# A hybrid block on one core: the table that orders the attention's steps on four engines is drawn anew

## What is computed

```python
x = x + attention(layernorm(x))   # gated delta rule, 16 heads of 128x128, short convolutions
x = x + ffn(layernorm(x))         # silu(x Wg) * (x Wu), 1024 hidden, then Wd
x = x + mamba(layernorm(x))       # 512 channels, 16 states, a scan over time
x = x + ffn(layernorm(x))
```

```python
q, k, v = (silu(short_conv(h @ W)) for W in (Wq, Wk, Wv))   # 4 taps; then q and k are normalised
g = exp(-softplus(h @ Wfa @ Wfb + dt_bias) * exp(A_log)); beta = sigmoid(h @ Wb)
# for every token t, with a 128x128 state S:
S = S * g[t]; delta = (v[t] - k[t] @ S) * beta[t]; S = S + outer(k[t], delta); o[t] = q[t] @ S
out = (rmsnorm(o) * norm_w * sigmoid(h @ Wga @ Wgb)) @ Wo
```

## Time and profile before

| | |
|---|---|
| median of three runs | 2769.22 us (2768.93 to 2771.27) |
| profiled execution | 2776.06 us |
| its span, first to last instruction | 2774.3 us |
| TensorE busy | 2495.6 us (90%), 46,512 matmul records |
| VectorE busy | 2124.1 us (77%) |
| ScalarE busy | 1393.4 us (50%) |
| GpSimd busy | 1260.3 us (45%) |
| mean granted TensorE clock | 0.966 |

### The profile page before, as it was taken

How to read it: one execution, slowest core, us unless ns; L and a number is a source line. 1 busy time by engine, 2 the same in 40 slices (tenths; PEclk the granted TensorE clock), 3 DMA queues, 4 the chain that set the end, 5 groups by cost and what they waited for, 6 DMA issues and landing times.

```text
span 2774.3 us, 102732 instructions
## 1 busy us (share of the span) xinstructions
PE 2495.6 (90%) x46512; PEld 1483.1 (53%) x46512; DVE 2124.1 (77%) x3249; ACT 1393.4 (50%) x2647; POOL 1260.3 (45%) x989
## 2 busy tenths in 40 slices
PE   6799999999999999999999999989878889888888
PEld 3466666666666566666666666664323333333333
DVE  3778888888888787888888877863229989999981
ACT  3445555455545455455555554533255645556342
POOL 0545545555555444555555454540014645546540
PEclk9899999999999999999999999999989999999999
DMA  1000000000000000000000000010012323323320
GB/s 52 22 12 14 13 20 13 15 13 20 13 16 13 13 20 13 16 13 20 13 15 15 18 13 15 7 52 1 25 38 92 126 92 112 112 90 127 121 95 15
DMA packets 52069, 105.61 MB, mean 38 GB/s; under 512 B 7084, under 2 KB 11948, under 8 KB 51376
## 3 DMA queue, kind: packets, MB, share of 16 engines
q1 hardware_dynamic: 51632, 99.04, 11.0%
HBM read 96.65 MB, written 2.37 MB: 36 GB/s over the span
## 4 chain that ended last, share of the span: by engine, by line
PE 60%; DVE 15%; issue 12%; ACT 11%; POOL 1%; DMA 1%; SPq 0%; DVEq 0%; ACTq 0%; POOLq 0%
PE bank L359 8%; PE bank L461 5%; DVE hs L1683 5%; PE bank L609 4%; PE bank L424 4%; PE pair L577 3%; PE bank L1500 3%; PE pair L567 3%; PE bank L393 2%; PE bank L583 2%; PE bank L549 2%; PE bank L531 2%; PE bank L1422 2%; PE bank L572 2%; DVE cv L651 2%
## 5 line engine op out<-in xcount | busy, mean ns | idle before, releaser
L1989 POOL TENSOR_TENSOR dBu<-dtu,Bn 128x1024 f32<-128x1024 f32 x128 | 306.2, 2394 | 232.1 <-DVE hc L1690 231.8
L651 DVE SCALAR_TENSOR_TENSOR cv<-raw,taps,cv 128x1024 f32<-128x1024 f32 x288 | 385.1, 1338 | 16.4 <-ACT cv L917 14.0
L359 PE MATMUL bank<-xn,W 128*128 128x512 f32 x768 | 381.9, 621 | 0.0
L1176 POOL TENSOR_TENSOR kL<-kL,tot 128x512 f32<-128x512 f32 x128 | 195.2, 1525 | 258.0 <-PE bank L424 258.0
L916 ACT ACTIVATE raw<-bank 128x512 f32<-128x512 f32 x192 | 114.9, 599 | 370.9 <-PE bank L359 370.1
L1500 PE MATMUL bank<-hc,eye 128*128 128x512 f32 x512 | 249.1, 615 | 56.2 <-DVE hc L1690 56.1
L1887 ACT ACTIVATE bank<-dtv,m_A 128x512 f32<-128x512 f32 x256 | 174.3, 687 | 209.6 <-DVE hs L1683 208.8
L1151 POOL TENSOR_TENSOR R<-qn,gate 128x1024 f32<-128x1024 f32 x32 | 108.6, 3393 | 269.5 <-ACT gate L977 269.5
L1500 PEld LDWEIGHTS bank<-hc,eye 128*128 128x128 f32 x512 | 93.7, 193 | 201.8 <-DVE hc L1690 110.6
L359 PEld LDWEIGHTS bank<-xn,W 128*128 128x128 f32 x768 | 132.3, 191 | 112.9 <-issue 103.0
L1690 DVE TENSOR_TENSOR hc<-hs,Cn 128x1024 f32<-128x1024 f32 x128 | 171.9, 1343 | 11.5 <-PE bank L1500 7.3
(11 more groups left out here) (267 smaller groups left out, 5657.4 us busy)
## 6 DMA issues: line engine op xcount, KB each, us to landing
Bn<-ssm_rows SPq DMA_DIRECT2D x128, 256.0 KB, 3.5
Cn<-ssm_rows SPq DMA_DIRECT2D x128, 256.0 KB, 3.2
W<-in_head_w SPq DMA_DIRECT2D x32, 448.0 KB, 3.3
WO<-in_out_w SPq DMA_DIRECT2D x32, 192.0 KB, 2.3
xT<-in_xT SPq DMA_DIRECT2D x1, 2048.0 KB, 8.1
out_xT<-xT SPq DMA_DIRECT2D x4, 512.0 KB, 3.8
xn<-in_w_gate SPq DMA_DIRECT2D x1, 1024.0 KB, 5.8
xn<-in_w_up SPq DMA_DIRECT2D x1, 1024.0 KB, 8.3
```

Of the source, the lines that this page charges most:

```text
L359: m = pe.matmul(psum[bank][:, :], w[:, (kind * KT + k) * P:(kind * KT + k + 1) * P], xn[:, k, b, cols], start=k == 0, stop=k == KT - 1)
L651: dve.scalar_tensor_tensor(cv[m % 2][:, :, :], raw[m % 2][:, :, i:i + SEG], taps[:, h, KQV[n], i:i + 1], cv[m % 2][:, :, :], MUL, ADD).the ...
L1176: pool.tensor_tensor(Lv[:, :, 0, :], Lv[:, :, 0, :], spread(two[:, :, 1], 2, half), MUL).then_inc(up_l.sem)
L1989: pool.tensor_tensor(dBu[at % AHEAD][:, :, :], dtu[s][:, half * DT2:(half + 1) * DT2, :], spread(Bn[at % DEEP][:, :], 1, DT2), MUL).then_i ...
```

## The change

`PLACES` gets other numbers. The thirteen rows keep their lags and their number of steps; nothing else in the kernel is touched. So every engine has the same instructions with the same waits, in another order within the attention. The order within a stage of one head can't change, only how stages and heads are braided.

```diff
 PLACES = [
-    (0, [-8.2, 14.4, 26.7, 27.6, 33.5, 34.5]),
-    (0, [27.6, 31.7, 37.1, 47.4, 51, 60.5]),
-    (0, [46.9, 51.8, 55.8, 62.6, 65.1, 65.1]),
-    (0, [67.1, 67.5, 78.1, 100.3]),
-    (0, [62.9, 63.5, 84, 86.2, 89.7, 93.9]),
-    (0, [81.3, 89.6]),
-    (1, [0.8, 4.1, 6.9, 15.2, 17.8, 24.6, 31.7, 31.7, 37.9, 46.9, 52.6, 53.3, 67.2, 70.5, 82.3]),
-    (1, [24.9, 28.9, 29.1, 34.9, 35.5, 37.3, 40.6, 48.9, 50.1, 54.1, 55.8, 56.3, 60.4, 67.8, 67.8, 70.4, 70.9,
-         84.5, 84.5, 88.1, 88.1]),
-    (1, [83.2, 84.6, 85.3, 86.5]),
-    (1, [99.2, 99.2, 106.9]),
-    (2, [10.8, 37.9]),
-    (2, [7.5, 13.7, 17.5, 19.7, 23.3, 28, 31.9, 35.9, 37.3, 47.4, 50.9, 53.2, 55.5, 57.8, 67, 69.4, 72.9,
-         73.7]),
-    (2, [34.2, 44.7, 81.3, 82, 85.1, 85.8, 86.3, 94.4, 105.8, 105.8, 107.2, 111.7, 122.8]),
+    (0, [2.5, 2.5, 24.8, 38.4, 41, 41.7]),
+    (0, [22.7, 39.6, 41.5, 44.3, 44.3, 48.4]),
+    (0, [41.8, 43.9, 51.9, 54.1, 57.4, 65.6]),
+    (0, [63.5, 69, 76.9, 102.8]),
+    (0, [52.6, 52.8, 78.8, 90.2, 96.9, 99.7]),
+    (0, [76.6, 91.5]),
+    (1, [-2, 1, 7.9, 12.8, 19, 21.2, 25.8, 26.9, 35, 37.9, 50.8, 59.7, 66.6, 71.4, 91.9]),
+    (1, [22.8, 27.7, 27.8, 29.2, 35.9, 40.2, 42.5, 52.2, 52.7, 55.4, 58.7, 59.2, 63.3, 66.6, 68.1, 71.2, 72.9,
+         87.8, 88.7, 93.4, 95]),
+    (1, [80.8, 80.8, 87.8, 89.9]),
+    (1, [103.1, 103.7, 106.9]),
+    (2, [12.1, 38.2]),
+    (2, [10.5, 13.1, 18.8, 19.2, 19.5, 25.4, 29.2, 36.8, 37.5, 42.5, 51.8, 53.9, 56.8, 60.5, 65.8, 70.2, 72.4,
+         72.5]),
+    (2, [37.6, 40, 77.7, 80.4, 82.2, 94.1, 97, 108.5, 108.6, 113.1, 116.1, 119.4, 127.1]),
 ]
```

## The result

On the chip and in the session that timed it, the changed kernel took 2784.11 us (median of 6 runs, 2781.87 to 2793.73) against 2770.58 us for the kernel before (6 runs): ratio 1.0051, 95% interval 1.0035 to 1.0066, 13.5 us. In a later session it took 2782.48 against 2776.24 us, ratio 1.0020, 0.9997 to 1.0044. The second interval just reaches 1, the first does not. So the new order is slower by some 6 to 14 us. The forecast was 56.8 us slower, within 2755 to 2885 us: the sign was right, the size about four times too large.

The account below looks back on a forecast made before the run. TensorE's own work sets the period, with stalls where it outruns its program's 256-instruction blocks. Terms -0.1 + 1.9 + 0.1 = +1.9 us per head, over 30 periods +57 us, bring the median from 2769.22 to 2826 us; range 2755 to 2885.

Parts of the forecast that it names:

- Steps between tiles: TensorE's 51 changes of tile per head stay 51, only their kinds differ: -0.1 us per head, bounds 0 and -0.2.
- The dense run: From the L424 behind the last L359 to the next L359: 1,526 instructions instead of 1,262, +1.9 us per head of stall.
- The first run: Small groups from L424 to L549, 590 instructions instead of 442: 0.5 us of stall as before, so 0.
- Waits on other engines: TensorE's waits for GpSimd, ScalarE and VectorE: +0.1 us per head in sum, bounds -0.2 and +0.6.
- what would show the prediction right: Issue idle before L461, L449, L377, L567 grows from 2.6 to about 4.5 us per head; stalls 256 instructions apart; busy time stays.
- (c): VectorE's L746 and L747 stand ahead of L870, and L689 ahead of L858: half of 0.2 us may go, -0.1.
- (a): An L424 waits for GpSimd's L1176 and L1178 with less TensorE work between: +0.2 us, counted to a third.
- (b): At the head's end L531 waits for a bank that ScalarE's L1027 frees later: +0.4 us, counted to a third.
- DMA: The loads of W, some 3 us earlier, and WO, 4 us later, still land in time: nothing.
- the falling clock: Rival: more and longer stalls lower TensorE's clock more often, 52 us more, 2878 us; chance 0.19.
- the clock kept up: Rival: long stalls go and TensorE's clock stays up, 52 us back; 2714 to 2771 us, middle 2743; chance 0.17.
- The fetch is hidden: Rival: TensorE's blocks arrive in time, stalls are of another kind and stay; 2763 to 2775 us, 2769; chance 0.12.

Follow-up runs that it names:

- the kernels with fewer instructions: L461's 32 products made 4 wider ones, 896 instructions less per head: 2687.27 us in the kernel before (ratio 0.9682), 2625.46 in the changed kernel (0.9459).
- the 32 added blocks: The kernel before with L377's group computed twice, 8,192 added instructions in all: 2901.66 us, ratio 1.0448.
- three parts of this one alone: The kernel before with only the new rows of products and inverse (2965.42 us), of out_gate, state and output (3119.26), or of the convolutions (3232.08).
- the two late L609: The kernel before with a head's last two L609 at places 167.3 and 172.5 instead of 111.7 and 122.8: 2767.24 us, ratio 0.9970.

## Why the prediction was right in sign and wrong in size

*Steps between tiles*, -0.1 us per head: busy time at full clock fell by 0.06. Right.

*The dense run*, +1.9: **this is the step that failed.** At full clock it is +0.41 (0.23 + 0.18), over all 25 heads +0.03, and "at 3.77 us a block it takes 22.5 us" is where it broke. The 3.77 was the mean of 18.60 us over 4.93 blocks, and so took the whole stretch between two L359 as held up by the fetch. Only its dense part is. Before, that part is 14.69 us for some 1,084 instructions (12 heads at full clock), 3.47 us per 256. The tail behind it, some 178 instructions in 4.23 us, runs at 6.1 us per 256 by its own work: its transposes take long enough for their few instructions that no stall is seen. With 3.47 the new dense part of 604 matmuls, some 1,220 instructions, wants 4.77 x 3.47 = 16.5 us; it has 16.31 - 2.87 = 13.44 of work, so about 3.1 us of stall, against 2.64: +0.5, measured +0.23 (+0.43 in the second profile of the same kernel, with 3.07). And L432, half a block of the sum, lies in the tail, where its 128 instructions found their block there: +0.18 at most, and none when it was moved alone. So one mean over a stretch with two limits made 1.9 out of some 0.4. The intervals from one stall to the next, where they are 256 instructions apart, could have told. The changed kernel has 44 in the attention: 19 of 3.45 to 3.48 us, 20 of 3.57 to 3.76, four of 4.0 and one of 8.1. The kernel before has 26: 16 of 3.45 to 3.75, and ten of 3.85 to 5.27, in all of which 0.15 to 0.27 of the DMA engines were busy with the load of W besides (0.12 at most in the others). The three that I quoted are of the ten. In six of the ten the wide L393 lie too, with 3.9 us of work or more, so that these six tell nothing of the load. The other four have 2.1 to 2.7 us of work and took 3.85 to 4.02, so the load may slow the fetch by some tenths of a us; it was not tried apart, and four of the changed kernel's intervals took 4.0 without it.

*The first run*, 0: **this step failed too, the other way.** The head's idle time outside dense part and tail rose by 0.24 at full clock (0.49 in the second profile) and by 0.52 over all 25 heads (0.58). Up to the dense part the stalls for issue rose from 0.27 to 0.68 us at full clock and from 0.13 to 0.87 over all 25, 0.93 in the second profile, much of it in front of L424 (19.3 us in all), a row that the kernel before does not have. The prediction read one head, in which the old run of 442 instructions had 0.5 us of stall, and took the cover of 1.2 us in front of it as fixed. With 590 instructions the run is stalled in more heads and for longer.

So the right sign is in part luck. The forecast had the extra stalls in the dense run and none in the first; over all heads the first run has most of them. Of what would show the prediction right, the stalls for issue did grow and stand 256 instructions apart, but to 3.5 us per head and not to 4.5.

*Waits on other engines*, +0.1 with bounds of -0.2 and +0.6: they fell by 14.0 us, 0.45 per head over all heads (0.09 over those at full clock), beyond the lower bound. The largest part is on VectorE, where the prediction had only (c): L577's wait for L827 went from 12.9 to 0.4 us. That it is because L746, L747 and L689 moved ahead was not tried apart. (a) is there once with 0.2 us, and (b) never. That the new order is better in this the kernels with fewer instructions showed too, by 31 of their 62 us.

*DMA*, nothing: right, TensorE waits for neither W nor WO.

*The clock*, taken as unchanged: 12 us less at the lower level, worth some 6. All of it is in the heads at the edges and the last two. In the 25 others the time at the lower level went from 61.4 to 75.1 us in one profile of the changed kernel and to 54.6 in the other. So neither clock rival came true: the falling clock asked for 52 us more, the clock kept up for 52 less.

*The fetch is hidden*: refuted by the 32 added blocks and their 124.5 us. The Trainium skill, "Runtime: NRT & Kernel Launch", section "Instruction fetch mechanics", has the block of 256 instructions as the page's queue counts it; that crossing one is mostly hidden does not hold in this kernel for blocks of less than some 3.5 us of work.

The sum with what was measured: the 25 heads are 16.3 us longer together (0.65 each, 0.55 of it idle time), the four at the edges 5.9 shorter and the last two (29 and 30) 3.1 shorter, which makes the attention's +7.3. Why the edges are shorter is open, and in the second profile the four are 2.3 longer. The medians' 13.5 and 6 us in two sessions show how far a single profile can be off.

What stays open is why the new table with L432 put back takes 2797 us and not 2784, if it does: the intervals of the ratios, 1.0047 to 1.0089 and 1.0035 to 1.0066, overlap. Its head at full clock takes 55.83 us, but so it does in the second profile of the changed kernel (55.82), and it has 92.2 us at the lower level against 85.3. For the old table with L432 ahead the account closes: 0.43 x 27 = 12 us of longer heads and 31 us more at the lower level, worth 15, against 19 us of the medians and 29 of the spans.

## What to carry to other kernels

When stalls "for issue" stand 256 instructions apart, calibrate the price of a block on a stretch that is stalled from end to end, and count only instructions that lie in it; what runs at its own slower pace behind it took half a block more for next to nothing here, a whole one not. Look at all runs of small groups and at many heads, for where a block begins moves from head to head. Count instructions as a resource of their own: 256 instructions there cost 3.6 times their work, in stalls and in the clock. And judge a table of places as a whole: each of three parts of this one alone cost 189 us or more, the whole 6 to 14.

## What the runs showed of the hardware

- Where nothing else limits TensorE, 256 instructions take 3.45 to 3.48 or 3.57 to 3.76 us (39 of 44 intervals of the changed kernel, 15 of the 20 longer ones at 3.73 to 3.76); 32 blocks more are 32 packets more in the page's q8.
- A block of 1.08 us of work added to a stretch limited by the fetch cost 3.9 us per head, a good part of it by the clock, which stood at its lower level for 184 us instead of 97. With the stalls for issue at half or less it stood there for 3 to 31 us, and a kernel with more idle time in short waits (the two late L609) kept its clock better than one with less idle time in long ones.
- The order that loses by 6 to 14 us with 46,512 matmul records wins by 62 us with 32,176.
